# Criss-cross attention on one core: where GpSimd adds the bias, and in what order VectorE works

## The reference

```python
q = einsum('oc,bchw->bohw', Wq, x) + bq;  k, v likewise
energy_H = einsum('bchw,bcgw->bhwg', q, k) - 1e30 * eye
energy_W = einsum('bchw,bchv->bhwv', q, k)
att_H, att_W = split(softmax(concatenate([energy_H, energy_W], -1)))
out = gamma * (einsum('bcgw,bhwg->bchw', v, att_H) + einsum('bchv,bhwv->bchw', v, att_W)) + x
```

## Time and profile before

| | |
|---|---|
| median of three runs | 3858.37 us |
| the profiled execution, its own time | 3862.07 us |
| its span, first to last instruction | 3860.3 us |
| TensorE (PE) matmul busy | 3709.9 us, 96% |
| VectorE (DVE) busy | 2951.6 us, 76% |
| ScalarE (ACT) busy | 1569.7 us, 41% |
| GpSimd (POOL) busy | 1351.2 us, 35% |
| HBM traffic over the span | 225 GB/s |
| granted clock of TensorE, mean | 0.992 |

### The profile page before, as it was taken

The page is one execution under the profiler, slowest core; times in us unless marked ns, Lnnn a source line. Parts: engine busy times, 40 slices in busy tenths (PEclk is TensorE's granted clock), DMA queues, the critical chain, the costliest instruction groups (busy, mean ns, idle before and its releaser), DMA issues.

```text
span 3860.3 us, 63621 instructions
## 1 busy us (share of the span) xinstructions
PE 3709.9 (96%) x24664; PEld 3360.4 (87%) x24664; DVE 2951.6 (76%) x4324; ACT 1569.7 (41%) x2322; POOL 1351.2 (35%) x984
## 2 busy tenths in 40 slices
PE   8799999999999999999999999999999999999999
PEld 7798888988889888898889988899888988889888
DVE  8767787688876888768887687877888668886655
ACT  7523444244542444424454244542445424454111
POOL 1432243322433225332253322533225233262333
PEclk9899999999999999999999999999999999999999
DMA  7687768777688776887769777597775977769765
GB/s 263 177 228 246 251 187 232 234 242 235 196 237 235 235 232 199 239 238 226 245 188 246 232 228 254 179 249 222 255 232 178 257 227 240 242 182 253 215 215 186
DMA packets 332792, 873.99 MB, mean 226 GB/s; under 512 B 34384, under 2 KB 182352, under 8 KB 332496
## 3 DMA queue, kind: packets, MB, share of 16 engines
q1 hardware_dynamic: 332496, 869.93, 74.9%
HBM read 662.18 MB, written 207.62 MB: 225 GB/s over the span
## 4 chain that ended last, share of the span: by engine, by line
PE 75%; DVE 18%; ACT 3%; issue 3%; DMA 0%; DVEq 0%; POOL 0%; SPq 0%; ACTq 0%; POOLq 0%
PE bank L1046 31%; PE bank L1013 18%; PE bank L1034 13%; PE bank L962 10%; DVE Sx L713 6%; DVE Sy L718 4%; PE bank L974 3%; DVE E L734 2%; DVE mx_c L729 2%; DVE zs_c L744 2%; DVE Y L799 1%; ACT Sx L568 1%; DVE Y L807 1%; ACT Q L577 1%; ACT Sy L604 1%
## 5 line engine op out<-in xcount | busy, mean ns | idle before, releaser
L1046 PE MATMUL bank<-Wv_hi,Sy 128*128 128x512 f32 x4608 | 1551.6, 400 | 0.0
L478 POOL TENSOR_TENSOR Y<-Y,gbv 128x1536 f32<-128x1536 f32 x192 | 696.3, 3627 | 1480.7 <-DMA Y<-in_x_pos 1480.7
L1046 PEld LDWEIGHTS bank<-Wv_hi,Sy 128*128 128x128 f32 x4608 | 872.2, 189 | 174.2
L1046 PE MATMUL bank<-Wv_lo,Sy 128*128 128x512 f32 x2304 | 904.3, 392 | 0.0
L1034 PE MATMUL bank<-Pt,XT 128*128 128x96 f32 x6144 | 740.8, 274 | 0.0
L1034 PEld LDWEIGHTS bank<-Pt,XT 128*128 128x128 f32 x6144 | 724.2, 192 | 10.0
L604 ACT ACTIVATE Sy<-Y 128x512 fp32r<-128x512 f32 x576 | 359.4, 627 | 830.3 <-PE bank L1046 776.1
L1013 PE MATMUL bank<-Pt,XT 128*128 128x96 f32 x6144 | 689.8, 276 | 1.0 <-issue 1.0
L1013 PEld LDWEIGHTS bank<-Pt,XT 128*128 128x128 f32 x6144 | 689.1, 193 | 1.2 <-issue 1.2
L713 DVE TENSOR_TENSOR Sx<-XA,Sx 128x768 fp32r<-128x768 f32 x348 | 488.4, 1444 | 237.5 <-ACT Sx L568 235.7
L807 DVE TENSOR_TENSOR Y<-bank,Y 128x512 f32<-128x512 f32 x576 | 390.1, 677 | 340.5 <-PE bank L1046 311.9
(11 more groups left out here) (71 smaller groups left out, 2660.7 us busy)
## 6 DMA issues: line engine op xcount, KB each, us to landing
XT<-in_x_col SPq DMA_DIRECT2D x384, 384.0 KB, 5.8
XT<-in_x_row SPq DMA_DIRECT2D x384, 384.0 KB, 6.7
Y<-in_x_pos SPq DMA_DIRECT2D x192, 768.0 KB, 6.2
out<-Y SPq DMA_DIRECT2D x184, 768.0 KB, 4.3
XA<-in_x SPq DMA_DIRECT2D x180, 768.0 KB, 6.5
e_scratch<-E SPq DMA_DIRECT2D x384, 144.0 KB, 2.1
Pe<-e_scratch SPq DMA_DIRECT2D x336, 144.0 KB, 6.5
XA_first<-in_x SPq DMA_DIRECT2D x12, 768.0 KB, 5.6
```

The source lines that it names most:

```text
L478: nc.gpsimd.tensor_tensor(at, at, gbv[:, :].unsqueeze(1).to_broadcast((P, TILES, C)), ALU.add)\
L1046: last = nc.tensor.matmul(proj_ps[k % 2][:, :], Sy[:, lo, ct, at], w[:, ct, :], start=(ct == 0 and lo == 0 and w is Wv_hi), stop=(ct == CT ...
```

## The change

Five edits, all in the order or the cut of work that was there before; nothing is computed differently.

1. `add_bias` becomes three instructions of 128x512 per chunk. The pieces of tiles 0 and 1 of chunk n+1 wait until `low_y(n+1, 1)` is done, that of tile 2 until `low_y(n+1, 2)` is. `finish` waits for its own piece. In the B part GpSimd takes two groups, then `scale` and the pieces 0 and 1, then two groups, piece 2, and the last group (before: three groups, `scale`, bias, two groups).
2. In VectorE's row stage the `shift` of column energies stands ahead of `low_y` and `sum_z`, and `low_y` of tile 2 stands ahead of the second `shift` of row energies.
3. ScalarE rounds the first half of an x chunk before `evict_kq`, and the second half after it.
4. The split of the value weights leaves VectorE's prologue: four pieces on ScalarE after groups 4, 6, 8, 10 of the first column stage, four low parts on VectorE after groups 5, 7, 9, 11. TensorE waits for them ahead of its first `project`.
5. `raw_v` is loaded near the end of the prologue's first half instead of at its start, and lies where `Sy` will be.

```diff
-            def add_bias(b, n):
+            def add_bias(b, n, t, after):
                 j = n % 2
                 pool.wait_ge(xres_in[j], past(xres_in[j], 16 * (b * (CHUNKS // 2) + n // 2 + 1)))
-                at = Y[:, out_slot(n), :, :].rearrange("p c n -> p (c n)").rearrange("p (t c) -> p t c", t=TILES)
-                nc.gpsimd.tensor_tensor(at, at, gbv[:, :].unsqueeze(1).to_broadcast((P, TILES, C)), ALU.add)\
-                    .then_inc(bias_added, 1)
+                pool.wait_ge(y_lo_made, past(y_lo_made, tile_no(b, n, after)))
+                nc.gpsimd.tensor_tensor(out_tile(n, t), out_tile(n, t), gbv[:, :], ALU.add).then_inc(bias_added, 1)
...
-                add_bias(b, 0)
+                for t in range(TILES):
+                    add_bias(b, 0, t, TILES - 1)
...
-                    for g in b_now[:3]:
-                        if g + 2 < CHUNKS:
-                            gather_k(b + 1, g + 2)
-                        mask(b + 1, g)
+                    for g in b_now[:2]:
+                        column_group(b + 1, g)
                     if n + 4 < CHUNKS:
                         scale(b, CHUNKS + n + 4)
                     if n + 1 < CHUNKS:
-                        add_bias(b, n + 1)
-                    for g in b_now[3:]:
-                        if g + 2 < CHUNKS:
-                            gather_k(b + 1, g + 2)
-                        mask(b + 1, g)
+                        add_bias(b, n + 1, 0, 1)
+                        add_bias(b, n + 1, 1, 1)
+                    for g in b_now[2:4]:
+                        column_group(b + 1, g)
+                    if n + 1 < CHUNKS:
+                        add_bias(b, n + 1, 2, 2)
+                    for g in b_now[4:]:
+                        column_group(b + 1, g)
...
                     if a_now:
+                        round_x(b + 1, a_now[1], (0,))
                         evict_kq(b + 1, a_now[0])
-                        round_x(b + 1, a_now[1])
+                        round_x(b + 1, a_now[1], (1,))
...
                 dve.wait_ge(proj_summed, past(proj_summed, k))
-                if t == 0:
-                    dve.wait_ge(bias_added, past(bias_added, b * CHUNKS + n + 1))
+                dve.wait_ge(bias_added, past(bias_added, k))
...
                     finish(b, n, 0)
-                    if after:
-                        low_y(b, n + 1, 0)
-                    if b_now and b_now[0]:
-                        sum_z(b + 1, CHUNKS + b_now[0] - 1)
                     if b_now:
                         shift(b + 1, CHUNKS + b_now[0])
+                        if b_now[0]:
+                            sum_z(b + 1, CHUNKS + b_now[0] - 1)
                     if turn_now:
                         sum_z(b + 1, 2 * CHUNKS - 1)
                         factors_of_columns(b + 1)
+                    if after:
+                        low_y(b, n + 1, 0)
...
-                    if a_now:
-                        shift(b + 1, a_now[0])
                     if b_now:
                         shift(b + 1, CHUNKS + b_now[1])
                     if after:
                         low_y(b, n + 1, 1)
-                    if b_now:
-                        sum_z(b + 1, CHUNKS + b_now[0])
+                    if a_now:
+                        shift(b + 1, a_now[0])
                     if attended:
                         add_row(b, n + 2, 0)
                         add_row(b, n + 2, 1)
+                    if b_now:
+                        sum_z(b + 1, CHUNKS + b_now[0])
...
                     finish(b, n, 2)
-                    if a_now:
-                        if a_now[1] + 1 < CHUNKS:
-                            low_x(b + 1, a_now[1] + 1)
-                        shift(b + 1, a_now[1])
-                    if b_now and CHUNKS - 1 not in b_now:
+                    last_group = b_now and CHUNKS - 1 in b_now
+                    if b_now and not last_group:
                         shift(b + 1, CHUNKS + b_now[3])
-                        sum_z(b + 1, CHUNKS + b_now[2])
+                    if a_now and a_now[1] + 1 < CHUNKS:
+                        low_x(b + 1, a_now[1] + 1)
                     if after:
                         low_y(b, n + 1, 2)
+                    if a_now:
+                        shift(b + 1, a_now[1])
...
-                dve.wait_ge(wv_in, 16)
-                nc.vector.tensor_copy(Wv_hi[:, :, :], raw_v[:, :, :]).then_inc(w_hi_made, 1)
-                dve.wait_ge(w_hi_made, 2)
-                nc.vector.tensor_tensor(Wv_lo[:, :, :], raw_v[:, :, :], Wv_hi[:, :, :].bitcast(F32), ALU.subtract)\
-                    .then_inc(w_lo_made, 1)
```

More of the change, by code:

```diff
@@ L24 @@
 PROLOGUE_PIECES = 3
+V_HI_GROUPS, V_LO_GROUPS = (4, 6, 8, 10), (5, 7, 9, 11)
 XRING = 6
@@ L109, in criss_cross_attention @@
         XT = sb("XT", [P, XRING, PIECE, C])
+        with ExitStack() as s3:
+            raw_v = sb("raw_v", [P, CT, C], F32, s3)
         Sy = sb("Sy", [P, 2, CT, CP], F32R)
@@ L485, in column_stage, with column_group @@
                     scale(b, g + PRING)
+            def column_group(a, g):
+                if g + 2 < CHUNKS:
+                    gather_k(a, g + 2)
+                mask(a, g)
             def zero_q(b):
@@ L553, in _, with round_x @@
                 act.sem_inc(s, START[s])
-            def round_x(a, m):
+            def round_x(a, m, hs=range(HALVES)):
                 if a == 0:
@@ L562, in round_x @@
                             out_landed(act, a - 1, slot)
-                for h, cts in enumerate(split_halves(a)):
+                for h in hs:
+                    cts = split_halves(a)[h]
                     if h == 0:
@@ L578, in evict_kq, with round_v @@
                     .then_inc(kq_evicted, 1)
+            def round_v(ct):
+                act.wait_ge(wv_in, 16)
+                nc.scalar.activation(Wv_hi[:, ct, :], raw_v[:, ct, :], ACT.Copy).then_inc(w_hi_made, 1)
             def exponentials(a, i):
@@ L631, in column_stage @@
                     move_column(b, g * ROWS + 3)
+                    if b == 0 and g in V_HI_GROUPS:
+                        round_v(V_HI_GROUPS.index(g))
             def row_stage(b, more):
@@ L653, in row_stage @@
                         exponentials(b + 1, a_now[0])
+                        if a_now[1] + 1 < CHUNKS:
+                            round_x(b + 1, a_now[1] + 1, (0,))
                         evict_kq(b + 1, a_now[1])
+                        if a_now[1] + 1 < CHUNKS:
+                            round_x(b + 1, a_now[1] + 1, (1,))
                     if more and n + 1 == A_FIRST:
                         round_x(b + 1, 0)
-                    if a_now and a_now[1] + 1 < CHUNKS:
-                        round_x(b + 1, a_now[1] + 1)
                     for g in b_now[1:3]:
@@ L719, in low_y, with low_v @@
                                         tile_of(Sy[:, 0, :, :], t).bitcast(F32), ALU.subtract).then_inc(y_lo_made, 1)
+            def low_v(ct):
+                dve.wait_ge(w_hi_made, 1 + ct + 1)
+                nc.vector.tensor_tensor(Wv_lo[:, ct, :], raw_v[:, ct, :], Wv_hi[:, ct, :].bitcast(F32), ALU.subtract)\
+                    .then_inc(w_lo_made, 1)
             def shift(a, i, before=True):
@@ L819, in column_stage @@
                     move_column(b, g * ROWS + 2)
+                    if b == 0 and g in V_LO_GROUPS:
+                        low_v(V_LO_GROUPS.index(g))
             def row_stage(b, more):
@@ L896, in row_stage @@
                         sum_z(b + 1, a_now[1])
+                    if b_now and not last_group:
+                        sum_z(b + 1, CHUNKS + b_now[2])
                     for g in b_now[4:]:
@@ L1059, in row_stage @@
                         attend_row(b, n, r)
+                if b == 0:
+                    pe.wait_ge(w_lo_made, 1 + CT)
                 for n in range(CHUNKS):
```

6 lines of the change are left out of this document (2 added, 4 removed).

## The result

| | before | after |
|---|---|---|
| median of four runs, same chip | 3857.11 us (3854.76 to 3863.48) | 3731.52 us (3730.29 to 3734.83) |
| ratio, 95% interval | 1 | 0.9673 (0.9656 to 0.9690) |
| span of the profiled execution | 3860.3 us | 3728.6 us |
| granted clock, mean | 0.992 | 0.995 |

The change is worth 126 us. The prediction was 3746, with a range of 3725 to 3790. The sign, the range and the mechanism (fewer and shorter stops of VectorE's low parts) held, and the forecast gain was 14 us too small.

A forecast was written before the change was run, and what follows sets the result against it. TensorE, 96% busy, bounds the kernel; only its waits, from VectorE low parts stopped beside GpSimd's bias, can go. 66 + 15 + 31 + 3 - 3 = 112 off 3862.1 gives 3750, 3746 for the runs' median; range 3725 to 3790.

The forecast's parts named there:

- A part: Row stage, first to last `project_kq` matmul: bias pieces avoid the low parts, 9.5 of 9.7 us a batch, 66 us (40 to 68).
- B part: Row stage, first to last column-energy matmul: 2.2 of 3.2 us lost per batch come back, 15 us (0 to 22).
- it closes barely: B part: GpSimd's loop through bias pieces, groups and the load of x takes 14 to 15 us against an iteration's 15.4.
- rival 1: B part: GpSimd's loop exceeds 15.4 us, TensorE waits for the fifth group's gather, 1 us in 35 iterations: 3796; chance 0.12.
- Turn: Last column energies to column attention: last `low_y` no longer stopped, clock stays 2.4 GHz, 4.4 us a batch, 31 us (20 to 34).
- Prologue: Before the first column `shift`: two value-weight instructions leave VectorE, TensorE's 3.07 us wait goes, 3 us (0 to 3.5).
- column stage: Taken back there: DMA share 1.04 barely keeps up and stages start some 4 us sooner, 0.4 a batch, minus 3 us.
- rival 2: Column stage runs dry, 3 us a batch go back, and the clock still falls at the turn: 3777; chance 0.15.
- Rival 3: A and B: `sum_z` and `turn` stop beside bias pieces instead, A and B give nothing: about 3830 to 3860; chance 0.03.
- Rival 4: B: loads of x land some 4 us above 6.2, each of 35 iterations loses 4: about 3900; chance 0.03.
- Rival 5: A part: stops weren't all on the path, slack of neighbours absorbs half the gain: 3779; chance 0.07.

The follow-up runs named there:

- Without the points: Kernel after, with the bias pieces' waits for `low_y` removed, each starting when its x has landed: 3732.58 us, ratio 0.9656.
- the run with longer groups: Kernel after, with the mask of each column group set twice, some 0.65 us more GpSimd time per group: 3798.32 us, ratio 0.9850.
- the cut alone: Kernel before, with the bias as three 128x512 pieces in a row in the old place, no waits between, `finish` waiting for the third: 3806.18 us, ratio 0.9869.
- the one-operand bias: Kernel before, with the bias instruction adding a constant instead of gamma*bv: 3837.92 us, ratio 0.9948.
- whole bias after its point: Kernel after, with the bias again one 128x1536 instruction, which waits for `low_y` of tile 1: 3766.76 us, ratio 0.9759.
- queries early: Kernel after, with the next batch's first two gathers of queries moved on ScalarE from n = 18 to the end of n = 17: 3718.55 us, ratio 0.9643.
- edit 3 undone: Kernel after, with ScalarE's order in the A part as before, x rounded whole after `evict_kq`: 3735.42 us, ratio 0.9679.
- edit 1 alone: Kernel before, with only the bias pieces, their waits, GpSimd's new order and `finish` waiting for its piece: 3734.31 us, ratio 0.9663.

## Why the prediction held, and where its sum was short

**A part, 66 predicted, 67.9 measured: right.** The floor of 201.5 us from the first to the last projection was 201.2, and every iteration is at its 17.47. The reason given for it was only half right. I argued tile by tile that each piece meets no low part because it waits for its point. Without the points the time is the same, and three pieces in a row in the old place do as well in A. What counts there, as far as these runs show, is that no stop is longer than VectorE's slack.

**B part, 15 predicted, 23.3 measured: a term mis-sized.** The step was "it closes barely [...] I take 2.2 of 3.2 a batch". The length of the loop fits: the run with longer groups puts it at 14 to 15 us. But a loop that closes costs nothing, however barely. Behind the first batch TensorE shows no wait for GpSimd, and 3.3 us a batch came, 23.3 in all, above my upper bound of 22. The discount mixed the chance that it doesn't close, which belongs in the rivals (rival 1), into the forecast.

**Turn, 31 predicted, 36.6 measured: two terms mis-sized, the mechanism right.** In batch 3 TensorE's stop fell by 3.3 us (predicted 3.4) and the clock stayed full, as I had chosen (1.5). I took off 0.5 for piece 2 meeting a step of the factors; it did (L786, 0.36 us), for 0.1 us. That the pieces don't meet the last `low_y` at all was wrong: it takes 0.97 to 1.48 us instead of 0.69, and TensorE stands for 1.12 to 1.64. The rest is that I worked from batch 3 alone. There the turn went from 16.0 to 11.1 us, 4.9. Three others took 16.9 to 17.3 in the kernel before, with a granted clock of 0.50 to 0.56 in the six microseconds from the end of the stop instead of 0.72, so they had more of it to win back. The mean over the seven is 5.2, above my upper bound of 4.9.

**Prologue, 3 predicted, 4.4 measured; column stage, -3 predicted, -0.8 measured.** The stages that start sooner find their first pieces of x with 10 to 12 us to spare instead of 15, and only batch 3 shows a stop, of 0.3 us; most of the rest is in the first column stage, which has the value weights beside it. A DMA share of 1.04 said that the queue is full, not that TensorE is waiting for it. The 4.4 of the prologue is above my bound of 3.5, but no better known than the spread of such starts allows (140.0 to 143.0 us with the old prologue, 136.9 to 138.4 with the new one, the kernel with longer groups left out).

**Rivals.** Rival 1 didn't happen, but 2 us more in GpSimd's loop bring it about. Of rival 2 the 0.3 us in batch 3 are seen; its other half, the clock, stayed at 1.00 in all seven turns. Rival 3 (other instructions stop instead) falls with 17.5 us in every A iteration. Rival 4 needed landings above 10 us; the time from issue to landing stayed at 6.2. Rival 5 fell with the floor.

**The rule of the Trainium skill** ("SBUF — State Buffer", rules for kernel authors: the second of the two to issue blocks until the first finishes). The prediction said that the trace disagrees, by one meeting at the turn, and overlooked what GpSimd was doing just before it:

```profile
2041.48 0.58 POOL L461 TENSOR_SCALAR_AFFINE_SELECT E<-E 96x384 f32<-96x384 f32 x1 [1.58 <-ACT E L583]
```

This mask starts 0.49 us ahead of `low_y` (2041.97) and ends 0.09 behind its start, and the bias follows straight behind the mask. So this isn't a meeting of two instructions, and `low_y` wasn't the first of the three. In the kernel before, a low part that started ahead of a bias, with no other GpSimd instruction under way, took its usual time in all 93 cases, one of them only 0.06 us ahead. One that started behind a bias was held in 147 of 149 cases; the other two met only its last 0.13 us. There the trace agrees with the page. It differs at the seven turns: by the rule `low_y` would be free at the mask's end, and the turn would give nothing. It was held through the bias as well, and the turn gave 36.6 us. Why is open: at 1199.16 and 2633.96 a `scale` was ending in the same way and the bias started 0.04 us behind `low_y`, which took its usual 0.68. In the cut alone the same mask stands at 2005.35, 0.49 us ahead of `low_y` (2005.84), and `low_y` takes 4.40 through three pieces. The same page's condition on the other side, a GpSimd instruction that reads SBUF, is met by the one-operand bias, which did stop `low_x` (4.84 us for two halves), and by the gather (0.92 us for `low_y`).

## What to carry to other kernels

An engine's busy time includes the time for which its instructions stand; look at the longest duration of a line beside its median, and at what the neighbour engine does in those microseconds. Here a long GpSimd instruction beside a VectorE instruction with both operands in SBUF was best cut so that each piece is shorter than VectorE's slack, with other GpSimd work between the pieces where low parts are due; waits for exact points were then not needed. An order of VectorE that does no harm in the cut kernel cost 33 us in the uncut one. Before two starts are compared, look at what the neighbour engine had under way. Where a stall stands just ahead of a dependent chain, as at the turn, price it once by itself: here one bias instruction of 24 held a quarter of the gain.

## What the runs showed of the hardware that I had not expected

- On GpSimd, adding a constant to 128x1536 float32 (one operand) takes 4.09 us in the median, against 3.5 for adding a second operand, and it stops VectorE's low parts too, though they end 0.33 us (`low_y`) or 0.07 (`low_x`) ahead of its record's end instead of 0.55 or 0.82 behind it. GpSimd's gather (a copy over 64 partitions, 0.86 us) stops them as well: `low_y` takes 0.92 to 0.97 us when it starts 0.48 behind one.
- The stop goes both ways. In the kernel before the bias takes 3.97 us instead of 3.48 when `low_y` starts 0.06 us ahead of it, and in the kernel after gathers become 1.44 to 1.83 us long.
- Between two GpSimd pieces in a row VectorE gets its turn after one piece in A (129 of 129, while the next one lengthens to 2.0 us), and never in B and at the turn (35 of 35, up to 4.40 us). The cause is open.
- Three pieces of 1.29 us take 3.8 to 3.9 us in place of 3.5: the cut costs GpSimd 46 us over the whole kernel (742.3 against 696.3 us for the bias, 0.08 per piece). Behind the first batch TensorE shows no wait for GpSimd in the kernel after.
- A stop of TensorE of 1.19 us at the turn left the granted clock of 1974 to 1979 us at 1.00. With a stop of 4.81, in the cut alone, that of the six microseconds behind it was 0.50, which is 1.2 GHz throughout. In between, the length of the stop alone doesn't tell: the clock stayed at 1.00 behind stops of 1.98, 2.00 and 2.31 us (whole bias after its point), and was 0.72 behind stops of 1.52 (queries early), 1.64 to 1.94 (edit 3 undone) and 1.81 (edit 1 alone).
